# Moving one batch's rotary rotation from GpSimd to VectorE in a two-layer attention and mixture kernel

## What is computed

```
x = x + tanh(g_xattn[0]) * L0_xattn(layernorm(x), ctx, ...)   # two-way cross attention with a gate
x = x + tanh(g_ffn[0])   * L0_ffn(layernorm(x), ...)          # 8 experts, top 1
x = x + tanh(g_xattn[1]) * L1_xattn(layernorm(x), ctx, ctx, ...)
x = x + tanh(g_ffn[1])   * L1_ffn(layernorm(x), ...)          # 8 experts, top 2
```

```
q = proj(query, Wq, bq); k = proj(key, Wk, bk); v = proj(value, Wv, bv)
q = q * cos + rotate_half(q) * sin
k = k * cos + rotate_half(k) * sin
attn_w = softmax(einsum('bhqd,bhkd->bhqk', q, k) * scale)
```

## Time and profile before

| what | value |
|---|---|
| median of 3 timed runs | 520.03 us (519.56 to 520.46) |
| the profiled execution's own time | 514.42 us |
| its span, first to last instruction | 513.1 us |
| mean granted clock of TensorE | 0.959 of full speed |
| busy: TensorE, VectorE, ScalarE, GpSimd | 470.4, 351.9, 338.1, 282.1 us |

### The profile page before, as it was taken

The page is one execution under the profiler, slowest core; times in us unless marked ns, Lnnn a source line. Parts: engine busy times, 40 slices in busy tenths (PEclk is TensorE's granted clock), DMA queues, the critical chain, the costliest instruction groups (busy, mean ns, idle before and its releaser), DMA issues.

```text
span 513.1 us, 11114 instructions
## 1 busy us (share of the span) xinstructions
PE 470.4 (92%) x3918; PEld 408.2 (80%) x3918; DVE 351.9 (69%) x873; ACT 338.1 (66%) x691; POOL 282.1 (55%) x362
## 2 busy tenths in 40 slices
PE   3999999989999968299987799999999999999996
PEld 3899999979988867186754488698797978888896
DVE  6757776697636764848555778776774785966485
ACT  3587888866666524344255588888778758688843
POOL 2435573675524386665278767846757454432264
PEclk9999999998999986689999699999999999999999
DMA  6999100112447432778847143130500503000001
GB/s 204 300 365 367 66 22 3 31 53 82 135 150 215 140 104 66 201 237 248 268 139 248 59 168 85 60 112 20 164 27 1 190 22 126 25 2 24 1 22 41
DMA packets 41783, 61.51 MB, mean 120 GB/s; under 512 B 5134, under 2 KB 22912, under 8 KB 41728
## 3 DMA queue, kind: packets, MB, share of 16 engines
q1 hardware_dynamic: 35872, 52.67, 32.4%
q0 software_dynamic: 1536, 4.20, 2.7%
q10 hardware_dynamic: 4320, 3.93, 2.2%
HBM read 26.21 MB, written 17.43 MB: 85 GB/s over the span
## 4 chain that ended last, share of the span: by engine, by line
PE 77%; DVE 6%; ACT 5%; issue 5%; POOL 4%; DMA 2%; SPq 0%; POOLq 0%; DVEq 0%; ACTq 0%
PE psum L382 16%; PE psum L384 14%; PE psum L383 14%; PE psum L615 6%; PE psum L549 6%; PE psum L389 4%; PE psum L586 4%; PE psum L603 4%; ACT PT L1355 2%; PE psum L550 2%; PE psum L539 2%; PE psum L624 1%; PE psum L560 1%; PE psum L423 1%; POOL yg L2790 1%
## 5 line engine op out<-in xcount | busy, mean ns | idle before, releaser
L2218 DVE TENSOR_REDUCE mpad<-psum 128x4 f32<-128x1024 f32 x64 | 76.6, 1219 | 22.1 <-PE psum L586 21.0
L1355 ACT ACTIVATE PT<-psum 128x1024 f32<-128x1024 f32 x64 | 64.1, 1024 | 21.3 <-PE psum L603 18.7
L2749 POOL TENSOR_TENSOR wA<-stage,wA 128x512 fp32r<-128x512 f32 x32 | 41.3, 1291 | 53.0 <-ACT wA L1402 50.6
L2287 DVE SCALAR_TENSOR_TENSOR xall<-psum,gat,xall 128x256 f32<-128x256 f32 x112 | 46.6, 476 | 7.1 <-PE psum L384 3.9
L382 PE MATMUL psum<-wB,wA 128*128 128x256 f32 x128 | 38.7, 302 | 0.0
L382 PE MATMUL psum<-x4h,wB 128*128 128x256 f32 x128 | 37.6, 294 | 0.0
L615 PE MATMUL psum<-PT,vv 128*32 128x256 f32 x512 | 36.0, 401 | 1.3 <-ACT PT L1355 1.3
L2736 POOL TENSOR_TENSOR parts<-qp,parts 128x512 fp32r<-128x512 f32 x16 | 20.8, 1299 | 29.6 <-ACT parts L1348 29.6
L383 PE MATMUL psum<-wB,wA 128*128 128x256 f32 x128 | 35.9, 281 | 0.0
L384 PE MATMUL psum<-wB,wA 128*128 128x256 f32 x128 | 35.8, 280 | 0.0
L384 PE MATMUL psum<-x4h,wB 128*128 128x256 f32 x128 | 35.8, 280 | 0.0
(11 more groups left out here) (284 smaller groups left out, 1751.5 us busy)
## 6 DMA issues: line engine op xcount, KB each, us to landing
st<-parts SPq DMA_DIRECT2D x48, 256.0 KB, 2.6
wt<-exp_d SPq DMA_DIRECT2D x30, 256.0 KB, 2.9
slots_d<-ys SPq DMA_DIRECT2D x3, 2304.0 KB
stage<-mats_d SPq DMA_DIRECT2D x21, 256.0 KB, 3.5
cx<-ctx_d SPq DMA_DIRECT2D x16, 256.0 KB, 3.3
qr<-qp SPq DMA_DIRECT2D x32, 128.0 KB
xs<-slots_d SPq DMA_DIRECT2D x30, 128.0 KB, 3.1
y_d<-ys ACTq DMA_DIRECT2D x30, 128.0 KB, 2.7
```

What stands on the lines that cost most here:

```text
L1355: e.activation(PT[:, i:i + 2, :, :].rearrange("p a k n -> p (a k n)"), ps2("ST", b, j).rearrange("p a n -> p (a n)"), ACT.Exp, scale=0.25) ...
L2218: e.tensor_reduce(mpad[:, :, 0:16].rearrange("p t (o a) -> p t o a", a=8)[:, :, :, j], ps2("max", b, j).rearrange("p o (t n) -> p t o n", ...
L2287: e.scalar_tensor_tensor(out=xall[:, b, t, :], in0=ps("dn", b, x)[:, t * 256:(t + 1) * 256], scalar=gat[:, b % 2, t, x:x + 1], in1=xall[:, ...
L2749: e.tensor_tensor(hlo[:, i, :], stage[:, n % 4, :], hh[:, i, :].bitcast(F32), ALU.subtract).then_inc(h_lo, 1)
```

## The change

Of batch 1, the second of the eight, the three operations of `turned` are issued by VectorE instead of GpSimd, for queries and for keys. In VectorE's list `turned(0, 1)` stands between `head_max(0, 0)` and `head_max(1, 0)`, and `turned(1, 1)` between `head_max(4, 0)` and `y_out(19)`. GpSimd keeps the subtraction for the low part at its place in its list. The order of TensorE's list stays; some of its PSUM bank numbers from tile 23 to the first `c_PV` are others.

```
-BY_POOL = 3
+BY_POOL = 3
+BY_VECTOR = 2
...
-            moe_T(23, 0)
-            ln_T("C", 3, 2)
+            moe_T(23, 2)
+            ln_T("C", 3, 3)
...
-            moe_T(24, 1)
-            c_v(2, 3)
+            moe_T(24, 0)
+            c_v(2, 1)
...
-            moe_T(25, 0)
+            moe_T(25, 2)
...
-            moe_T(26, 3)
-            c_maxT(0, 2)
+            moe_T(26, 1)
+            c_maxT(0, 3)
...
-            c_qk(3, 1, 0)
+            c_qk(3, 0, 2)
...
-            moe_T(28, 2)
+            moe_T(28, 3)
...
-            c_PV(0, 0, 2)
+            c_PV(0, 0, 1)
...
-            def turned(i):
+            def turned(i, b):
-                w.wait_ge(a_qp, 2)
+                n = 2 * b + i + 1
+                w.wait_ge(a_qp, 2 * b + 2)
                 w.wait_ge(d_tab, TABS)
-                w.wait_ge(d_qr, 64)
+                w.wait_ge(d_qr, 64 * (b + 1))
+                w.wait_ge(r_add, n - 1)
                 e.tensor_tensor(qp[:, i, :, :], qp[:, i, :, :], rope[:, 0:1, :].broadcast_to([128, 2, 256]), ALU.mult).then_inc(r_cos, 1)
                 e.tensor_tensor(qr[:, i, :, :], qr[:, i, :, :], rope[:, 1:2, :].broadcast_to([128, 2, 256]), ALU.mult).then_inc(r_sin, 1)
-                w.wait_ge(r_cos, i + 1)
-                w.wait_ge(r_sin, i + 1)
+                w.wait_ge(r_cos, n)
+                w.wait_ge(r_sin, n)
                 e.tensor_tensor(qp[:, i, :, :], qp[:, i, :, :], qr[:, i, :, :], ALU.add).then_inc(r_add, 1)
...
             head_max(0, 0)
+            turned(0, 1)
             head_max(1, 0)
             head_max(2, 0)
             head_max(3, 0)
             x_lo("C", 2)
             y_out(18)
             head_max(4, 0)
+            turned(1, 1)
             y_out(19)
             y_out(20)
             st1_init()
...
             def turned(i, b):
                 n = 2 * b + i + 1
-                if b >= 1:
+                if b >= BY_VECTOR:
+                    w.wait_ge(r_add, n - 1)
                     w.wait_ge(a_qp, 2 * b + 2)
```

More of the change, by code:

```diff
@@ L2467, in vector_program @@
             alloc(1)
-            turned(0)
-            turned(1)
+            turned(0, 0)
+            turned(1, 0)
             x_lo("C", 1)
```

## The result

The changed kernel is slower: 525.27 us in the median of 6 runs (522.23 to 527.29), against 519.91 us of the kernel before, a ratio of 1.0122 (95% interval 1.0087 to 1.0158). By the ratio that is 6.3 us; the two medians are 5.4 us apart. The forecast was 2.1 us and 522.1 us, with a range up to 524.7. All ratios here leave out runs that were more than 1.5% above the fastest of their kernel: one of e4's twelve (656.13 us) and two of e13's twelve (525.93 and 527.15 us), beside two of the kernel before.

A forecast was written before the change was run, and what follows sets the result against it. TensorE was taken to bound the kernel; its overlapping delays of 0.8, 1.4 and 2.0 us, plus some 0.1 us on ScalarE, made 2.1 us. Added to 520.03 us this gave 522.1 us, range 518.0 to 524.7.

The forecast's parts named there:

- What bounds the kernel: TensorE sets the end; a microsecond it loses in the stretch of the change is lost at the end.
- What the edit removes: GpSimd loses six operations, 7.6 us of work, but gives nothing back by being free.
- What it adds: VectorE gets the six operations, at 2.0 us a set with GpSimd quiet.
- The price of 2.6 us for meeting one GpSimd operation: On VectorE, each set that meets a GpSimd operation costs 2.6 us more, 4.6 instead of 2.0 us.
- First set: Ahead of `head_max(1, 0)`: `c_max(3, 0)` waits 1.6 us, half of it covered, and TensorE is 0.8 us late.
- Second set: Ahead of `y_out(19)`: memsets 3.2 us late; TensorE 1.4 us late at `ln_T` of batch 3, 2.0 at `moe_T(26)`.
- 1.2 us of loss at the far end: Copies of `stack(1)` land at 250.8, before `c_max(0, 1)` at about 251.2; the latest landing would cost 1.2 us.
- the slots of tile 26: Queued behind the copies, they land at 253.4 and make `moe_T(26)` 2.0 us late, bounds 1.4 to 3.3.
- the sum: Delays on TensorE overlap: 0.8, 1.4, then 2.0 us, plus some 0.1 on ScalarE, giving 2.1 us.
- one more dip: Rival: another half-clock stretch in the waits the edit opens, at 3.8 us, giving 525.9 us; chance 0.08.
- The faster rival: Rival: arriving 2 us later, the stretch at 287 to 297 us keeps its clock, saving 3.8 us: 518.3 us; chance 0.22.
- The sign of being wrong: The prediction is wrong if `moe_T(26)` is not late, or is late and the dip near 290 us has gone.

The follow-up runs named there:

- e4: The changed kernel with the two memsets of `st1_init` moved ahead of `y_out(15)`, into VectorE's idle time at 221 us; ratio 1.0038 to the kernel before.
- e13: The kernel before, rotation on GpSimd, with the copies of `stack(1)` held back until TensorE has done `moe_w(22)`; ratio 1.0048 to the kernel before.
- e1: The kernel before with only the rotation of batch 1's queries moved to VectorE, new bank numbers kept; ratio 1.0021 to the kernel before.
- e5: The changed kernel run and profiled once more, nothing else altered; ratio 1.0125 to the kernel before.
- e6: The changed kernel with seven dummy matmuls on TensorE in the wait of `c_max(0, 1)` for `stack(1)`; ratio 1.0043 to the kernel before.
- e2: The kernel before with only the rotation of batch 1's keys moved to VectorE; ratio 1.0096 to the kernel before.
- e8: The kernel before with the two memsets of `st1_init` moved ahead of `y_out(15)`, into VectorE's idle time; ratio 0.9974 to the kernel before.
- e9: The kernel before with both the changed kernel's PSUM bank numbers and the early memsets, rotation on GpSimd; ratio 0.9979 to the kernel before.
- e7: The kernel before with the changed kernel's PSUM bank numbers, rotation on GpSimd; ratio 0.9976 to the kernel before.
- e10: e9 with 22 dummy matmuls in TensorE's waits between the third `c_exp` of batch 0 and that of batch 1; ratio 0.9978 to the kernel before.
- e12: e10 with 40 more dummy matmuls in TensorE's waits at 189, 205 and 210 us; ratio 0.9987 to the kernel before.
- e3: The changed kernel with all PSUM bank numbers of the kernel before; ratio 1.0076 to the kernel before.
- e14: e13 with seven dummy matmuls in the wait of `c_max(0, 1)` for the late copies; ratio 1.0043 to the kernel before.

## Why the prediction was wrong

**What bounds the kernel** held in the main: what TensorE had lost by the first `c_exp` came out at the end within some 3 us (0.71 in the profile and 1.1 by time in e1, 6.54 and 6.5 in e5, 2.79 and 2.2 in e6, but 2.03 and 5.0 in e2). Loss and time are of different executions, so closer agreement is in part luck. The whole profile after is 7.8 us longer than that of before (520.9 against 513.1): 1.57 ahead of the stretch, 3.83 in it, and 2.4 behind it. The last isn't shown to be the edit's. From the first `c_exp` to the end it is 251.3 us in the kernel before and 253.7 here, but 253.9 and 253.2 in e8 and e9, where the rotation is on GpSimd.

**What the edit removes** was right, nothing came back.

**What it adds** was right: 2.0 us a set, as forecast, with GpSimd quiet. No new operation met GpSimd. The price of 2.6 us for meeting one GpSimd operation was misread, without consequence: VectorE's 3.26 us from 210.99 on spanned two of them, that of the earlier trace rows at 212.42 and this one ahead of it in the kernel before:

```profile
211.20 1.27 POOL L2709 TENSOR_TENSOR cl<-cx,ch 128x512 fp32r<-128x512 f32 x1
```

**First set**: a loss of 0.8 us was forecast, 0.71 was measured (e1), and the wait for VectorE was 1.47 us against 1.6.

**Second set**: the memsets were forecast 3.2 us late and were 2.9. The wait of `ln_T` was there with 0.28 us. The place of the next wait was wrong: the forecast had the copies of `stack(1)` landed when `c_max(0, 1)` came, "with 1.2 us of loss at the far end", and the slots of tile 26 late. Instead `c_max(0, 1)` waited 1.49 us, and `moe_T(26)` behind it then waited for nothing. Two sizes were off. The six copies took 4.57 us to issue and not 3.85. And the forecast took the middle of six landings, 2.7 us, where `c_max(0, 1)` waits for all six: the last went out at 250.1 and TensorE started at 253.87, 3.8 us later, which is near the far end of 4.3. The waits together cost 2.64 us up to `moe_w(25)` in the first profile and 2.54 in e5, where 2.0 was forecast at this place, inside the 1.4 to 3.3. That it came inside is luck in part, since the bounds were those of another transfer. With the waits alone, the kernel would have been at 520.03 + 2.6 = 522.6 us, inside the range.

**The step that failed** is the clock behind the new waits, which the sum put at nothing. It is the rival *one more dip*. It was named, with a price of 3.8 us, and given 0.08 because the waits "are 1 us long in a stretch that is else full". The full stretch did not keep the dip away; it made the dip cost time. The dip cost 1.19 us in the profile after and 4.00 us in e5, and filling the wait took away 4.3 us by time (e6). So the sum is 2.5 us of waits and 4.0 of half clock, 6.5 us, against 6.3 and 6.5 measured. The price in the rival was right, and its chance wrong.

**The faster rival** priced the dip between 287 and 297 us at 3.8 us by the durations of single matmuls, and expected it to stay or to go as a whole. The sign of being wrong that was named with it decides nothing: `moe_T(26)` was 3.7 us late, and that dip had neither gone nor moved by 2 us. The profile after has 3.4 us at half speed at 278 to 282 us and 6.9 at 294 to 303, together 10.3 where the kernel before has 10.2. These dips lie elsewhere without the edit, too (e7, rotation on GpSimd: 6.8 us, from 274 to 282; e8: 13.6 in two pieces), so that one execution says little of them. In e10 and e12 a higher clock there gave nothing that could be measured.

Open is why the half speed lasts 3.4 us in one execution of the changed kernel and 10.2 us in another, why waits of 1.0 and 1.3 us were followed by none in the profiles of e2 and e13, and what makes some 2 of the 5.0 us that e2 costs by time, and whether the new bank numbers take part in the size of the dip (e3).

## What to carry to other kernels

When a full stretch of TensorE gets a new wait, price it twice: the wait, and the same matmuls at 1.2 GHz behind it (here 2.5 and 4.0 us). Look for what is queued behind the moved work on its new engine (here two memsets that held six copies), and move what has no hurry into idle time first; that took away more than half of the loss. When a step waits for several copies, price it by the last landing and not by the middle one. A wait that can't be removed can be filled with dummy matmuls into a bank that is already taken. That gained 4.3 us in the changed kernel (e6), nothing measurable where the late copies stood alone (e14), and nothing where TensorE often idles anyway (e10, e12).

## What was unexpected of the hardware

- A wait of 1.42 us in an otherwise full stretch was followed by 10.2 us at half clock (e5), and with 1.83 us of dummy matmuls in its place by none (e6). A wait of 1.74 us was followed by 3.4 us (e3). Waits of 1.02 us (e2's profile) and 1.31 us (e13's) were followed by none in those executions.
- The mean granted clock and the time don't go together in general: 0.975, with dummies, and 0.955, without, gave the same time within 0.13% (e12).
- The same six copies took between 3.85 us (the kernel before) and 4.76 us (e14) to issue, by one of the six that took up to 1.51 us where the others took 0.6. Going out later isn't the whole of it: e3's went out as late as the changed kernel's and took 3.87 us, and e8's took 4.37 us though they were not late.
